# Attention and routed FFN on one core: the exponentials of blocks 4 and 5 turned by VectorE and DMAs instead of TensorE

## What is computed

```python
x = x + xattn(layernorm(x), ctx)       # softmax(q k^T / sqrt(128)) v
h = layernorm(x)
scores = where(rank(probs) < sampled_k, probs, 0)      # 8 experts
for e in range(8):
    out += scores[e] * down[e](silu(gate[e](h)) * up[e](h))   # 336 hidden
x = x + out
```

## Time and profile before

| | |
|---|---|
| median of 3 runs | 751.24 us (751.12 to 753.06) |
| span of the profiled execution | 749.5 us |
| TensorE busy | 740.2 us (99%) |
| VectorE busy | 628.6 us (84%) |
| GpSimd busy | 578.4 us (77%) |
| ScalarE busy | 552.9 us (74%) |
| DMA queue of SP | 24.4% of 16 engines |
| granted TensorE clock, all slices | full (9 of 9) |

### The profile page before, as it was taken

The page is one execution under the profiler, slowest core; times in us unless marked ns, Lnnn a source line. Parts: engine busy times, 40 slices in busy tenths (PEclk is TensorE's granted clock), DMA queues, the critical chain, the costliest instruction groups (busy, mean ns, idle before and its releaser), DMA issues.

```text
span 749.5 us, 13834 instructions
## 1 busy us (share of the span) xinstructions
PE 740.2 (99%) x3721; PEld 366.3 (49%) x3721; DVE 628.6 (84%) x1395; ACT 552.9 (74%) x978; POOL 578.4 (77%) x620
## 2 busy tenths in 40 slices
PE   8999999999999999999999999999999999999998
PEld 5544454544445445454544545445454544544445
DVE  7899888898888888788888888888888887978777
ACT  5998787776877776777776777776777767777664
POOL 2686979789796877969689696886968688687764
PEclk9999999999999999999999999999999999999999
DMA  9200412204032132312224132132313212120110
GB/s 349 66 24 1 84 30 57 58 14 97 25 78 56 49 79 55 84 41 69 70 40 95 40 81 62 42 83 54 82 43 69 72 28 56 32 58 11 28 30 29
DMA packets 107271, 45.40 MB, mean 61 GB/s; under 512 B 86872, under 2 KB 97112, under 8 KB 107224
## 3 DMA queue, kind: packets, MB, share of 16 engines
q1 hardware_dynamic: 106792, 44.39, 24.4%
q10 hardware_dynamic: 432, 0.48, 0.2%
HBM read 26.46 MB, written 10.78 MB: 50 GB/s over the span
## 4 chain that ended last, share of the span: by engine, by line
PE 94%; ACT 3%; DVE 2%; issue 1%; POOL 0%; DVEq 0%; ACTq 0%; POOLq 0%
PE bank L634 28%; PE bank L635 28%; PE bank L636 28%; PE bank L544 2%; PE bank L517 2%; PE bank L630 1%; PE bank L528 1%; PE bank L593 1%; PE bank L612 1%; PE bank L771 1%; DVE bank L1562 0%; ACT up_hi L829 0%; DVE hid_lo L1568 0%; ACT down_hi L829 0%; ACT k_early L890 0%
## 5 line engine op out<-in xcount | busy, mean ns | idle before, releaser
L1207 POOL TENSOR_TENSOR weighted<-silu,score_bc 128x512 f32<-128x512 f32 x336 | 430.9, 1298 | 89.0 <-ACT silu L972 86.2
L1562 DVE SCALAR_TENSOR_TENSOR bank<-bank,h_scale,weighted 128x512 f32<-128x512 f32 x336 | 253.5, 754 | 94.6 <-PE bank L636 76.2
L966 ACT ACTIVATE hid_hi<-bank 128x512 f16<-128x512 f32 x336 | 200.9, 598 | 155.4 <-DVE bank L1562 154.6
L972 ACT ACTIVATE silu<-bank,silu_scale 128x512 f32<-128x512 f32 x336 | 230.7, 687 | 24.3 <-PE bank L636 24.1
L1568 DVE TENSOR_TENSOR hid_lo<-bank,hid_hi 128x512 f16<-128x512 f32 x336 | 227.5, 677 | 0.0
L634 PE MATMUL bank<-xn_lo,gate_hi 128*128 128x512 f16 x336 | 127.5, 379 | 1.1 <-ACT silu L972 1.1
L634 PE MATMUL bank<-xn_lo,up_hi 128*128 128x512 f16 x336 | 127.4, 379 | 1.2 <-DVE hid_lo L1568 0.9
L635 PE MATMUL bank<-xn_hi,up_lo 128*128 128x512 f16 x336 | 127.3, 379 | 0.0
L636 PE MATMUL bank<-xn_hi,up_hi 128*128 128x512 f16 x336 | 127.3, 379 | 0.0
L636 PE MATMUL bank<-xn_hi,gate_hi 128*128 128x512 f16 x336 | 127.3, 379 | 0.0
L635 PE MATMUL bank<-xn_hi,gate_lo 128*128 128x512 f16 x336 | 127.3, 379 | 0.0
(11 more groups left out here) (200 smaller groups left out, 780.3 us busy)
## 6 DMA issues: line engine op xcount, KB each, us to landing
x_in<-in_x SPq DMA_DIRECT2D x16, 256.0 KB, 2.8
y_kept<-y_sb SPq DMA_DIRECT2D x60, 64.0 KB, 2.6
y_tok<-y_kept SPq DMA_DIRECT2D x15, 256.0 KB, 2.8
out<-out_sb SPq DMA_DIRECT2D x15, 256.0 KB, 2.2
xt_in<-in_x_t SPq DMA_DIRECT2D x14, 256.0 KB, 2.8
row_bc<-row_kept SPq DMA_DIRECT2D x14, 256.0 KB, 3.7
ctx_in<-in_ctx_t SPq DMA_DIRECT2D x14, 240.0 KB, 2.7
p_kept<-y_sb SPq DMA_DIRECT2D x10, 256.0 KB, 2.0
```

The lines of the kernel that those rows point to most:

```text
L966: af(hid_hi[j % HRING][:], up_bank[j % U_BANKS][:], ACT.Copy).then_inc(hid_hi_ready, 1)
L972: af(silu[j % RING][:], gate_bank[(par + j) % G_BANKS][:], ACT.Silu, scale=silu_scale[:])\
L1207: g.tensor_tensor(weighted[j % RING][:], silu[j % RING][:], score_bc[par][:], ALU.mult)\
L1562: v.scalar_tensor_tensor(up_bank[j % U_BANKS][:], up_bank[j % U_BANKS][:], h_scale[:], weighted[j % RING][:], ALU.mult, ALU.mult).then_inc ...
```

## The change

```diff
-FIRST_SQUARES = LOOP_FIRST + 2
+FIRST_SQUARES = LOOP_FIRST
```

## The result

| | before | after |
|---|---|---|
| median of 12 runs | 751.21 us (751.12 to 753.18) | 753.18 us (752.69 to 754.57) |
| ratio | | 1.0024, 95% interval 1.0016 to 1.0032 |
| span of the profiled execution | 749.5 us | 751.2 us |

The change costs 2.0 us in the runs and 1.7 us on the profiled spans: under 0.3%, but the interval leaves no doubt of its sign. The page hardly shows it: VectorE's busy time grows by 0.2 us, and TensorE's falls by 0.7.

What follows compares the result with a forecast made beforehand. TensorE bounds, with VectorE's chain tying at one place of each turn. (0.64 VectorE delay + 0.2 attend wait) x 2 = +1.7 us, span 749.5 to 751.2; from the median 751.24, predicted 752.9 us, range 751.4 to 754.1.

Steps and rivals of the forecast that it cites:

- VectorE's chain: Turns 2 and 3: block transpose delays low(9) and low(10), so up(13) starts at 152.26 instead of 151.62, +0.64 us per block.
- Price of the block transpose: VectorE, iteration 10 between hidden(10) and low(9): the added instruction makes everything queued behind it 0.64 us later.
- the transposes' 0.44 us: TensorE, 148.46 to 148.90: four transposes per block removed, -0.44 us per block if nothing else moved, -0.9 in all.
- The wait at attend: Iteration 15 of turns 2 and 3: attend reached at 155.51, data at 155.73, a wait of 0.2 us per block.
- The landing: Probabilities through the DMAs: data signalled 7.65 us after the block transpose starts, last packets at 7.15 plus 0.5.
- a third of the slice: Write of p_kept, turn 4: last packets read as about 237.67, next issue at 238.16, so the signal comes 0.5 us later.
- The rule against the change: Receipt 2 us behind the last packet: data at 9.15 us, each attend waits 1.7, +4.7 us, 755.9; 0.01 of second rival's chance.
- Turn 3 repeats turn 2.: Turns 2 and 3, blocks 4 and 5: each sum is made for turn 2 and doubled, (0.64 + 0.2) x 2 = +1.7 us.
- All turns from turn 4 on keep their length.: Changed profile, turns 4 to 15: no change of length; otherwise something else is at work that these steps don't have.
- The bound of 8.35 us: Block 15's attend, 8.35 us after its block transpose, didn't wait; data that late in turn 2 would mean a 0.9 us wait.
- the gain on TensorE: First rival: VectorE's delay is hidden and the transposes are a gain, -0.9 to 0 us, 750.3 to 751.2; chance 0.07.
- The transfers: Second rival: attend in iteration 15 of turns 2 and 3 waits for DMAs over 0.48 us, up to 754.3 us; chance 0.14.

Runs made afterwards that it cites:

- VectorE's instruction alone: Kernel before plus VectorE's block transpose of probabilities in turns 2 and 3, result unused, TensorE's transposes kept: turn 2 44.66 us, turn 3 44.89, span 750.9.
- the kernel with everything moved: Changed kernel, blocks 4 and 5: row_sum behind low(11), attend at the end of iteration 15, block transpose behind low(9); 751.53 us against 751.41, ratio 1.0001.

## Why the prediction was right

Forecast 752.9 us, measured 753.18; 751.2 for the span, measured 751.2. The mechanism in turn 2 was right; that the sum came out as closely as it did is in part luck, as two of the steps show:

- **VectorE's chain.** Price of the block transpose 0.64, measured 0.63 (147.87 to 148.50). The up product of tile 12 was put 30.00 us after the turn's first gate matmul and came at 29.95, that of tile 13 at 32.80 and came at 32.75. The mechanism is shown by VectorE's instruction alone (+0.59), and that the transposes' 0.44 us are worth nothing is shown by the kernel without them (0.00).
- **The wait at attend.** 0.2 per block was forecast; 0.26 came in turn 2, none to speak of in turn 3. The landing was put at 7.65 us after the block transpose; the changed kernel's was 7.54 in turn 2, and the eleven regular ones of the kernel with attend in iteration 14 are 7.27 to 7.73. The 0.11 too much came from a wrong reading: "a third of the slice" is the mean busy share of 16 DMA engines and says nothing of when the last packet ended. In finer slices of the kernel before it is after 237.70, not at 237.67:

```profile
237.70:237.80 0.10, 0.10 (x1) 0.00 (x0) 0.10 (x1) 0.10 (x2) 0.00 (x0) 1.00 0.09 21
237.80:237.90 0.10, 0.10 (x2) 0.02 (x1) 0.10 (x1) 0.10 (x1) 0.07 (x1) 1.00 0.00 0
```

So the next issue (238.16) follows by 0.4 us, not 0.5. On the other side the sum lacked a term: an attend that has waited takes 0.10 more for its eight matmuls (1.16 against the 1.06 of the earlier trace rows). The wait ahead of it was 0.16.

- **The rule against the change.** The Trainium skill, in "DMA: Bandwidth & Descriptors", section "Anatomy of one DMA — SWDGE (gpsimd) path", puts most of about 2 us of fixed cost behind the last byte. That section is on transfers issued by GpSimd, and these are issued on the SP queue; for them the traces don't agree: p_kept's next step comes 0.4 us after its last packet, attend 0.36 to 0.53 after that of the loads, and eleven of the twelve landings are under 7.8 us, not 9.15.
- **"Turn 3 repeats turn 2."** This was wrong, and two errors cancelled by luck. Turn 3's +0.82 is 0.59 of VectorE's delay and 0.23 of the hole, with no wait at attend: in that turn of the changed kernel the data were there when attend was due, 7.39 us after the block transpose. That isn't a property of turn 3: other kernels have landings of 7.27, 7.38 and 7.44 there. 0.84 was forecast per turn; 0.85 and 0.82 came, the second for another reason than I gave.
- **"All turns from turn 4 on keep their length."** True of turns 4 to 12. Turn 13 took 0.19 more, through the late write. The prediction said that a changed length there would mean something else at work, and did not say what could be. I had costed the removed instructions at their time on the engine alone, and not asked what their absence shifts. The bound of 8.35 us, from the earliest attend that had not waited, was no bound for other kernels: block 15's data now came at 8.44 and held its attend.

The rivals: the gain on TensorE did not come, and the kernel with everything moved shows how little of it there was. The transfers did not decide: their part is 0.26 of the 1.67 us of turns 2 and 3, and 0.19 in turn 13. By the runs the change is 1.97 us slower, 0.3 above the span's difference, which the spread of the runs of each kernel (over 1.8 us) covers.

## What to carry to other kernels

Before counting work taken off the busiest engine as a gain, look at what its next step waits for: here 0.44 us of transposes stood in front of a wait, and removing them was worth 0.00, though the engine was 99% busy. When work is moved to an engine with spare time on the average, find the stretch where it has none; a second chain that ties with the first pays for every instruction put into it, and only behind the last thing that is waited for is it free. An asynchronous path that runs well in most turns may do so because something else stands in front of its consumer; measure its landing by putting the consumer early.

## What the runs showed of the hardware

One VectorE instruction added in idle time cost 0.23 us 26 us later in straight-line code (turn 3, 44.07 to 44.30), and another 0.24 in turn 12 with one added but not with two. Gaps of 0.2 to 0.4 us, for which the trace names no wait, stood ahead of other instructions once one or two had been added; in turn 14, where they met slack, they cost nothing. Eight matmuls taken out in turns 2 and 3 moved an instruction queue's 16 KB packet into a data write 450 us later, which then took 2.75 to 3.3 us instead of 2.0; putting them back undid it. A chain of one block transpose, one write of 256 KB to DRAM and four loads in runs of 128 bytes landed 7.3 to 7.7 us after its start, in the loop and outside it, and the consumer started 0.36 to 0.53 us after the last packet.
